# Two seams of a four-stage transformer kernel: the scan's first tile computed in the feed-forward stage, the mixture's first group in the scan's tail

## What is computed

```python
# layer 0
h = layernorm(x) * (1 + ca) + sa ; x = x + ga * linear_attention(h)
h = layernorm(x) * (1 + cb) + sb ; x = x + gb * (sparse_2to4(silu(h @ w_gate) * (h @ w_up)) @ w_down)
# layer 1
h = layernorm(x) * (1 + ca) + sa
k, v = rope(h @ Wk.T), h @ Wv.T              # 16 heads of 16
def step(W, kv):                             # 64 blocks of 16 tokens, in series
    z = kc @ W
    return W - kc.T @ ((z - vc) * inv_n), z
x = x + ga * (layernorm(zs) * gamma + beta) @ Wo.T
h = layernorm(x) * (1 + cb) + sb             # 8 experts, the top 2 weighed, and a shared part
x = x + gb * (routed(gelu(h @ w1 + b1) @ w2 + b2) + shared(h))
```

## Time and profile before

| | us |
|---|---|
| median of three runs | 1066.62 |
| the three runs | 1062.79, 1066.62, 1066.68 |
| profiled execution, its own time | 1061.99 |
| its span | 1060.0 |
| busy in it: TensorE / VectorE / ScalarE / GpSimd | 995.6 / 678.6 / 332.5 / 250.2 |
| mean granted TensorE clock | 0.986 |

### The profile page before, as it was taken

The page is one execution under the profiler, slowest core; times in us unless marked ns, Lnnn a source line. Parts: engine busy times, 40 slices in busy tenths (PEclk is TensorE's granted clock), DMA queues, the critical chain, the costliest instruction groups (busy, mean ns, idle before and its releaser), DMA issues. The chain is left out here.

```text
span 1060.0 us, 15726 instructions
## 1 busy us (share of the span) xinstructions
PE 995.6 (94%) x6016; PEld 800.8 (76%) x6016; DVE 678.6 (64%) x1494; ACT 332.5 (31%) x604; POOL 250.2 (24%) x319
## 2 busy tenths in 40 slices
PE   6899999999999999999779999977999997999997
PEld 4688888888888888888668888864666664887875
DVE  6766676666676666666648887562667763466556
ACT  4343333343433333433224232102132421422220
POOL 2222222222221222222010100123344633111011
PEclk9999999999999999999999999998999999999999
DMA  9300000000000000000030000002544430000000
GB/s 293 134 2 1 1 1 1 1 1 2 1 1 1 1 1 1 2 1 1 20 124 10 1 1 1 1 1 44 139 128 97 87 72 7 1 16 16 11 21 20
DMA packets 33051, 33.37 MB, mean 31 GB/s; under 512 B 6857, under 2 KB 26834, under 8 KB 32978
## 3 DMA queue, kind: packets, MB, share of 16 engines
q1 hardware_dynamic: 32978, 32.38, 11.0%
HBM read 23.98 MB, written 8.13 MB: 30 GB/s over the span
## 5 line engine op out<-in xcount | busy, mean ns | idle before, releaser
L393 POOL TENSOR_TENSOR rope_sum<-rope_cos,rope_sin 128x512 f32<-128x512 f32 x80 | 114.9, 1436 | 257.2 <-DVE rope_sin L514 257.2
L429 ACT ACTIVATE rope_exp<-rope_sum 128x512 f32<-128x512 f32 x80 | 50.5, 631 | 205.5 <-POOL rope_sum L393 205.4
L783 PE MATMUL proj<-wo_sb,attn_out_t 128*128 128x256 f32 x512 | 113.2, 379 | 0.7 <-issue 0.7
L783 PEld LDWEIGHTS proj<-wo_sb,attn_out_t 128*128 128x128 f32 x512 | 96.1, 190 | 13.4 <-issue 0.9
L732 PE MATMUL num<-v_ones,score_masked 128*128 128x129 f32 x512 | 100.2, 278 | 5.9 <-DVE score_masked L572 5.9
L733 PE MATMUL num<-state,q_t 128*128 128x129 f32 x512 | 99.9, 277 | 0.0
L1910 DVE SCALAR_TENSOR_TENSOR m_acc<-m_expert,gates,m_acc 128x256 f32<-128x256 f32 x128 | 61.9, 484 | 49.0 <-PE m_expert L1991 42.2
L732 PEld LDWEIGHTS num<-v_ones,score_masked 128*128 128x128 f32 x512 | 83.0, 193 | 13.4 <-DVE score_masked L572 8.0
L511 DVE TENSOR_TENSOR rope_cos<-proj,cos_sb 128x512 f32<-128x512 f32 x80 | 55.3, 691 | 52.5 <-PE proj L686 52.5
L686 PE MATMUL proj<-w_hi,a_h_hi 128*128 128x512 f32 x192 | 79.4, 494 | 4.0 <-DVE w_lo L136 2.1
L733 PEld LDWEIGHTS num<-state,q_t 128*128 128x128 f32 x512 | 78.6, 194 | 0.0
(11 more groups left out here) (218 smaller groups left out, 1905.3 us busy)
## 6 DMA issues: line engine op xcount, KB each, us to landing
kv_scratch<-t_kv SPq DMA_DIRECT2D x16, 256.0 KB, 2.5
kv_rows<-kv_scratch SPq DMA_DIRECT2D x32, 128.0 KB, 3.5
a_stage<-in_wqkv SPq DMA_DIRECT2D x6, 512.0 KB, 5.5
wo_sb<-in_wo SPq DMA_DIRECT2D x1, 2048.0 KB, 9.4
a_stage<-in_wgu SPq DMA_DIRECT2D x4, 512.0 KB, 9.6
out<-x_sb SPq DMA_DIRECT2D x16, 128.0 KB, 1.7
u_scratch<-u_rows SPq DMA_DIRECT2D x28, 64.0 KB, 2.8
t_u<-u_scratch SPq DMA_DIRECT2D x14, 128.0 KB, 2.1
```

Of the source, the lines that this page charges most:

```text
L393: pool.tensor_tensor(y[:, parity], t1[:, parity], t2[:, parity], ALU.add).then_inc(s["y_done"], 1)
L783: mm = pe.matmul(proj[:, b, 0:D], o_t[:, i, :], wo[:, i, :], start=(i == 0), stop=(i == H - 1))
```

## The change

Three things are done. (1) The chain of the scan's first tile, up to the write to `kv_scratch`, is written into `ffn_phase`: norm statistics at the last group's block m = 6, transposition and projection in PSUM of the feed-forward stage between `pe_gates` and the last `down`, rope into buffers of that stage, and the DMA out on SyncE at the end of its stream. `t_kv`, `kv_scratch` and the semaphores of it are shared by both stages. In `scan_phase` those pieces are gone, the first memset of `kv_rows` covers a quarter of it, a second one comes later, and `keep_warm(4)` ahead of step 0 becomes 2 + 1. (2) All of the mixture's g = -1 turn stands in the scan's tail, between the pieces of the last two tiles; `keep_warm(8)` and `keep_warm(2)` are gone. The hidden blocks land in `kv_ps`, logits and turned gates in `z_ps`, the next group's transposition in `g_ps`, the activations in `m_act0`, which also serves as staging for `w1` earlier. The mixture's loop begins at g = 0. (3) The groups are taken in the order `TURNS = (0, 2, 1, 3)`: the second group is then tiles 8 to 11, which are finished before the last scan tiles are; group 1 of before (tiles 4 to 7) holds the last tile.

```diff
@@ ffn_phase, GpSimd, ScalarE, VectorE, TensorE, SyncE
-                for g in range(NG):
+                for g in range(NG - 1):
...
+                add_rows(NG - 2, range(GT - 1))
                 for b in range(B):
                     scan_rstd(pool, b, 1)
+                add_rows(NG - 2, range(GT - 1, GT))
+                for b in range(B):
+                    pool.wait_ge(t["hi_done"], b + 1)
+                    pool.tensor_tensor(t_lo[:, b], t_h[:, b], t_hi[:, b].bitcast(F32), ALU.subtract).then_inc(t["hl_done"], 1)
...
+                act.wait_ge(msem["mod_done"], 1)
+                for b in range(B):
+                    act.wait_ge(t["xn_turned"], B)
...
                 act_gates(act)
+                for b in range(B):
+                    act.wait_ge(t["proj_full"], b + 1)
+                    act.wait_ge(t["rope_done"], b + 1)
...
+                        if g == NG - 1 and m == NM - 2:
+                            dve.wait_ge(s["x_done"], NC + 1)
+                            for b in range(B):
+                                scan_norm(dve, 0, b)
...
+                for b in range(B):
+                    scan_centre(dve, 0, b, 1)
                 dve.wait_ge(msem["mod_full"], 2)
...
+                for b in range(B):
+                    dve.wait_ge(t["proj_full"], b + 1)
...
                 dve_gates(dve)
...
+                for b in range(B):
+                    pe.wait_ge(t["xn_done"], b + 1)
+                    for k in range(KD):
+                        i = pe.transpose(turn[:, 1, b * D + k * P:b * D + (k + 1) * P],
+                                         self.t_xn[:, b, k * P:(k + 1) * P], ident[:])
+                    i.then_inc(t["xn_turned"], 1)
                 pe.wait_ge(s["hid_done"], NG * NM)
                 pe_gates(pe)
+                for b in range(B):
+                    pe.wait_ge(t["hi_done"], b + 1)
+                    pe.wait_ge(t["hl_done"], b + 1)
...
+                            mm = pe.matmul(gate[:, b, :], hh[:, b, k], ww[:, k, WKV:WKV + 2 * D],
...
+                for b in range(B):
+                    sp.wait_ge(t["kr_done"], b + 1)
+                    sp.wait_ge(t["v_kept"], b + 1)
+                    sp.dma_start(self.kv_dram[0, b], kv[:, 0, b].rearrange("p k u e -> p (k u e)")
+                                 ).then_inc(t[f"kv_out{b}"], 16)
@@ scan_phase, GpSimd
-                pool.memset(kv_r[:], 0.0).then_inc(zeroed, 1)
+                pool.memset(kv_r[:, 0, :, 1], 0.0).then_inc(zeroed, 1)
...
+                e_rstd(pool, 1)
+                self.ratio_of(pool, 0)
                 for b in range(B):
                     keep_z(NC - 1, b)
                 for b in range(B):
+                    z_rstd_of(NC - 1, b)
+                for b in range(B):
                     add_rows(NC - 2, b)
@@ scan_phase, ScalarE
+                self.gelu(act, 0, 0, kv_ps)
+                for b in range(B):
+                    drain_out(NC - 2, b)
+                for m in range(1, 4):
+                    self.gelu(act, 0, m, kv_ps)
+                self.gates_turned(act, 0, z_ps)
+                self.drain_group_norm(act, 1, g_ps)
+                self.gelu(act, 0, 4, kv_ps)
+                for b in range(B):
+                    drain_out(NC - 1, b)
+                for m in range(5, NH):
+                    self.gelu(act, 0, m, kv_ps)
@@ scan_phase, VectorE
+                self.clear_gates(dve)
...
+                e_norms(dve, 1)
+                self.gating(dve, 0, z_ps)
+                e_centre_group(dve, 1)
                 for b in range(B):
                     z_norm(NC - 1, b)
...
+                self.split_group(dve, 1)
                 for b in range(B):
                     out_rows(NC - 1, b)
@@ scan_phase, TensorE
-                keep_warm(4)
+                keep_warm(1)
...
-                pe.wait_ge(u_done, NC * NMB)
-                keep_warm(8)
...
+                self.hidden(pe, 0, 0, kv_ps)
+                pe.wait_ge(u_done, NC * NMB)
+                self.logits(pe, 0, z_ps)
+                self.hidden(pe, 0, 1, kv_ps)
+                last_rows(NC - 2)
+                for m in range(2, 4):
+                    self.hidden(pe, 0, m, kv_ps)
+                self.gates_turn(pe, 0, z_ps)
+                self.turn_group(pe, 1, g_ps)
+                self.hidden(pe, 0, 4, kv_ps)
+                out_turn(NC - 1)
+                self.hidden(pe, 0, 5, kv_ps)
+                last_rows(NC - 1)
+                for m in range(6, NH):
+                    self.hidden(pe, 0, m, kv_ps)
@@ moe_phase
-                for g in range(-1, NG):
+                for g in range(NG):
```

More of the change, by code:

```diff
@@ L45 @@
 E, EH = 8, 128
+NH = E + 2
 GT = 4
 NG = NT // GT
+TURNS = (0, 2, 1, 3)
 WCH = 512
@@ L1642, in gradient, with keep_warm @@
                     mm.then_inc(g_full, 1)
+                def keep_warm(times):
+                    for _ in range(times):
+                        pe.matmul(z_ps[:], ident[:], wo[:].rearrange("p k d -> p (k d)"), start=True, stop=True)
                 for j in range(U):
@@ new lines, in gates_turn, with hidden @@
+    def gates_turn(self, pe, g, small):
+        s, gates = self.moe_s, self.e_gate["gates"]
+        pe.wait_ge(s["gates_done"], g + 1)
+        for i in range(GT):
+            t = pe.transpose(small[:, i * P:(i + 1) * P], gates[:, g % 2, i, :], self.ident[:])
+        t.then_inc(s["gturn_full"], 1)
+    def hidden(self, pe, g, m, hid):
+        s, n = self.moe_s, g * NH + m
+        w_hi, w_lo, h_hi, h_lo = self.w_hi, self.w_lo, self.e_h_hi, self.e_h_lo
+        if n >= 2:
+            pe.wait_ge(s["act_done"], n - 1)
+        cols = slice(m * P, (m + 1) * P)
+        for i, (ww, hh) in enumerate([(w_hi, h_hi), (w_lo, h_hi), (w_hi, h_lo)]):
+            for k in range(KD):
+                mm = pe.matmul(hid[:, n % 2, :], ww[:, k, cols], hh[:, g % 2, k, :],
+                               start=(i == 0 and k == 0), stop=(i == 2 and k == KD - 1))
+        mm.then_inc(s["hid_full"], 1)
```

367 lines of the change are left out of this document (187 added, 180 removed).

## The result

The changed kernel takes 1034.95 us (median of 4 runs, 1031.37 to 1039.71) against 1064.7 for the kernel before on the same chip (4 runs, 1060.33 to 1066.68): ratio 0.9722, 95% interval 0.9686 to 0.9758. On another chip the same pair gave 1034.77 and 1063.17, ratio 0.9732 (0.9719 to 0.9745). The forecast was 1036.0, its range 1029 to 1045. The profiled execution took 1031.37 us, its span is 1029.6.

The account below looks back on a forecast made before the run. It took the chains holding two seams, the scan's start and its tail, as the bound, not TensorE's 94% busy share. Gains 0.5 + 12.9 + 2.7 + 14.5 = 30.6 us gave 1036.0 against the median, range 1029 to 1045.

Parts of the forecast that it names:

- End of the feed-forward stage: Feed-forward end: added TensorE products fit in idle time and `f_dx` comes earlier; gain 0.5 us, bounds 0.8 and -3.2.
- the walk: The prediction's link-by-link timing of engines, waits and transfers at both seams, from which its gains were taken.
- The wait that should have vanished: Sign of being right: TensorE's wait of 2.92 us before the last `f_rows` piece is gone.
- Start of the scan: Scan's start to step 0: T + 6.3 in place of T + 19.2; gain 12.9 us, bounds 15 and 9.
- Rival (c): Scan's start: `kv_rows` reads issued together take twice as long, feed-forward end absorbs nothing; 3.9 + 3.7 less, 1043.6 us; chance 0.06.
- Clock: Steps 0 to 3 of the recurrence: clock full in place of low; gain 2.7 us, bounds 0 and 2.7.
- Tail: Last step to group 1's first block: TensorE's list replaces idle products and waits; gain 14.5 us, bounds 16 and 6.
- The slack of 0.7: Scan's tail: the last tile's norm chain could be 0.7 us late before TensorE loses time.
- rival (b): Scan's tail: the last tile's norm chain holds it, gain 8 in place of 14.5 us; 1042.5 us; chance 0.09.
- The sum: All four gains, 0.5 + 12.9 + 2.7 + 14.5 = 30.6 us, taken from the profiled execution's 1061.99.
- Rival (e): Recurrence: clock low throughout, 4.06 us per step, 1.73 more than at full; 1077 us at 24 steps; chance 0.03.

Follow-up runs that it names:

- Two queues: Changed kernel with the first tile's second pair of `kv_rows` reads on ScalarE's queue and gate clearing behind the second tile's centring: 1034.3 us, ratio 0.9721.
- The full clock on the kernel before: Kernel before with `keep_warm(4)` ahead of step 0 made `keep_warm(8)`, eight idle products more: 1068.55 us, ratio 1.0044.
- the kernel with the projection twice: Changed kernel with the twelve projection products at the end of the feed-forward stage issued twice: 1041.2 us, ratio 0.9792.

## Why the prediction was right, point by point

*End of the feed-forward stage, 0.5: measured 0.70.* The last `f_rows` starts at 702.24 where the walk had it at 704.0 in the time of before, 702.2 with the 1.78 taken off. That they meet is luck in part: in the walk TensorE's list set this start and `f_dx` had 0.9 us to spare, while in the profiles `f_dx` sets it, 0.9 later than the walk had it. The chain to it was put together differently. VectorE's choice came 1.07 later, because `beats` took 4.77 us beside GpSimd's `f_h_lo` where it took 3.69 before; and the stretch from the choice to the gate operations shrank by 1.76. The wait that should have vanished is 1.15 at full clock and 0.16 at low: the twelve products and a low clock take from the same idle time. The rule of the Trainium skill (SBUF — State Buffer, Who interferes with whom) that was weighed there, on a VectorE instruction with two SBUF inputs, fits `beats`, which reads SBUF twice, and has nothing to say on the gate operation that it was applied to: that one reads PSUM and took 1.22 beside the rope sums, as in the earlier trace rows. `beats` took 4.75 to 4.77 us in every profiled execution with `f_h_lo` beside it, and 3.69 in the four without.

*Start of the scan, 12.9: measured 11.65.* This is the term that was mis-sized most, inside its bounds of 15 and 9, and of its two chains the walk had the wrong one end last. The reads, forecast for T + 6.0, were counted from the issue of the second pair at 4.2 us, the figure of a lone pair; they took 5.7 with all four on their way and let step 0 go at T + 7.58. The engines' side, forecast for T + 6.3, was through at T + 6.72. VectorE's wait of 2.58 is not the distance between the two, since it counts from VectorE's own last work: faster reads could win some 0.8 here. That the reads hold step 0 is shown by the run without idle products, where it stands at T + 7.6 all the same. Two queues brought it to T + 7.24. Rival (c) had the right mechanism, at a third of the 3.9 us it was given for this term.

*Clock, 2.7: measured 2.87 in steps 0 to 3, and 1.06 given back.* The reason given was incomplete in two ways. It named the long wait that is gone and the products in the rest of the stretch side by side; the first isn't enough, for without the idle products the clock falls and costs 8.9 us. And the gain isn't kept whole, because the next tile's reads set a second pace beside the steps: behind SyncE's order write, read, write, read a recurrence that runs faster waits at the tiles' ends. The full clock on the kernel before shows it bare: 2.7 us won in three steps, nothing in the recurrence as a whole, and all of it kept once the writes go first.

*Tail, 14.5: measured 14.15.* Waits of 0.34, 0.29 and 0.20 stand for the 0.4, 0 and 0.6 of the walk, and the end came 0.4 later. The slack of 0.7 given to the norm chain was not there: it is 0, since VectorE takes the group's centring first. So rival (b) was close, and a list that is shorter ahead of `out_turn` wins nothing here as long as the norm comes no sooner.

*The sum.* 30.6 was forecast against the profiled execution's own time. The same stretches give 28.3, 2.3 less; the two spans differ by 30.4 only because 1.78 lie ahead of the change and 0.31 behind it, which is luck. In the medians it is 29.8. Of the signs named for being right two failed: the wait of 2.92 is 1.15 and not gone, and step 0 stands at 7.6 and not at 6 to 7. Of the signs of being wrong one appeared, that of (c): a wait over 2 us of `u_rows` on the reads. Rival (e) had its price per step right (4.06), and a part of it is real: a low clock within the recurrence appeared in the kernel with the projection twice, behind late transfers, which its text did not name. In the two profiled executions of the changed kernel the longest such wait behind step 0 is 1.81 and 1.84 us, at step 24, and no low clock follows.

*What stays open.* How late each read is depends on the next tile's own chain (norm, rope, write) and on SyncE's order; only the order was varied. The low clock behind a late transfer was seen in the slowest run of the doubled projection, behind two of its three waits over 2 us; the typical run, 4.1 us in excess, was not profiled, and what decides whether such a wait lets the clock fall is not settled. A norm moved ahead of the centring in the tail was not tried.

## What to carry to other kernels

A serial stage has a second pace beside its own: the transfers that bring the next piece. Whoever speeds up the steps or starts them sooner should look at once at the queue that feeds them, and put every write that nothing holds ahead of the first read that waits for one. Where a stall is removed at a seam, keep idle products in what is left of it until a run without them shows that they can go. And where an engine's list shows only short waits, that list need not be the only bound: shorten it once by some products and see whether the time follows.

## What the runs showed of the hardware

Six idle products, 2.9 us, decided on 8.9: without them TensorE ran at the 1.2 GHz level from 716 to 740, though from 722 on the profile has it busy all the time. A late transfer can let the level fall within the recurrence, but does not always: VectorE's waits of 2.54 and 2.15 us were followed by it, one of 2.62 at step 24 of the same execution and the 2.72 of the warm kernel before were not. Four reads of `kv_rows` under way together took 4.8 to 5.4 us from the last issue to use, a lone pair 3.4. And `t_zn`, with one tensor and two columns from SBUF, took 0.82 us beside a GpSimd addition in the tail of the changed kernel and 0.42 just before:

```profile
876.40 0.42 DVE L1534 TENSOR_SCALAR t_zn<-t_z,t_mv,t_rstd 128x256 f32<-128x256 f32 x1
...
877.20 1.47 POOL L1370 TENSOR_TENSOR x_sb<-x_sb,t_dx 128x256 f32<-128x256 f32 x2
...
877.26 0.82 DVE L1534 TENSOR_SCALAR t_zn<-t_z,t_mv,t_rstd 128x256 f32<-128x256 f32 x1 [0.45 <-POOL t_rstd L1357]
```

The price isn't fixed: beside the same kind of addition the two `t_zn` at 863.28 and 864.11 (the second only in part beside it) took 0.55 and 0.45.
